# A float32 layer pair on one core: an interleaved order for the last two units' second products, and another refinement of the inverse square root

## What is computed

```python
# layer 1
approx_up = x @ up_w.T                              # 128 columns
delta = x @ gate_w.T - local_point
out = approx_up @ local_approx_output.T + sum over m = 1..6 of
      (delta**m / m! * approx_up) [m > 4: only where |delta| <= 2.5] @ fuse_weight[:, :, m-1].T
out += (silu(x @ ffn_gate_w.T) * (x @ ffn_up_w.T)) @ ffn_down_w.T      # 1248 inner columns
x = layernorm(x + out)                              # (x - mean) / sqrt(var + 1e-5)
# layer 2
inter = x @ c1_w.T @ c2_w.T                         # 1792 columns in 56 blocks of 32
idx = argmax in each block                          # one row of w1 and w2t is chosen per block
x = layernorm(x + relu(x @ w1[idx].T) @ w2t[idx])
```

## Time and profile before

| | us |
|---|---|
| median of 3 executions | 782.3 (782.02 to 784.47) |
| the profiled execution, as a whole | 782.61 |
| its span | 780.7 |
| TensorE (PE) busy | 753.7 |
| VectorE (DVE) busy | 480.8 |
| ScalarE (ACT) busy | 226.4 |
| GpSimd (POOL) busy | 159.4 |
| mean granted TensorE clock | 0.996 of full |

### The profile page before, as it was taken

One profiled execution on the slowest core, in us unless ns is written; L12 is line 12 of the kernel. 1 busy time (PEld: TensorE's weight loads), 2 busy tenths in 40 slices (PEclk: granted clock), 3 DMA queues, 4 the chain that ended last, 5 costly groups with the idle time before them and its releaser, 6 DMA issues.

```text
span 780.7 us, 12799 instructions
## 1 busy us (share of the span) xinstructions
PE 753.7 (97%) x3814; PEld 356.6 (46%) x3814; DVE 480.8 (62%) x854; ACT 226.4 (29%) x356; POOL 159.4 (20%) x132
## 2 busy tenths in 40 slices
PE   7999999999999999999999999999999999999994
PEld 2444443444444444444444444454545444444441
DVE  4888677697867777767967786445654561034105
ACT  1644456437432222222122222221222222112220
POOL 0444433111111111111111112212211221222210
PEclk9999999999999999999999999999999999999998
DMA  8446328210000000000000000000100010001001
GB/s 324 173 163 200 55 53 302 77 54 1 1 1 0 0 1 0 0 0 0 0 3 0 0 1 1 1 1 1 54 0 0 0 55 0 0 1 55 0 0 54
DMA packets 9341, 31.81 MB, mean 41 GB/s; under 512 B 992, under 2 KB 1632, under 8 KB 8416
## 3 DMA queue, kind: packets, MB, share of 16 engines
q1 hardware_dynamic: 7200, 27.22, 9.2%
q0 software_dynamic: 2112, 4.19, 3.2%
HBM read 27.22 MB, written 4.19 MB: 40 GB/s over the span
## 4 chain that ended last, share of the span: by engine, by line
PE 83%; DVE 8%; issue 3%; ACT 2%; DMA 1%; SPq 1%; DVEq 0%; ACTq 0%; POOL 0%
PE acc L366 28%; PE pa L354 19%; PE pb L354 19%; PE acc L431 9%; PE pick_b L462 1%; DMA big<-in_x_t 1%; DVE big L1229 1%; PE pick_a L452 1%; PE pick_a L414 1%; DVE big L943 1%; DVE small L1155 1%; PE pa L568 1%; ACT big L788 1%; PE pick_a L470 1%; PE pb L568 1%
## 5 line engine op out<-in xcount | busy, mean ns | idle before, releaser
L366 PE MATMUL acc<-big,work 128*128 128x512 f16 (+1 forms) x1128 | 254.6, 379 | 0.0
L853 POOL TENSOR_TENSOR work<-work 128x512 f32 (+1 forms) x96 | 115.9, 1207 | 533.1 <-ACT work L759 287.9
L354 PE MATMUL pa<-xs,big 128*128 128x512 f16 (+1 forms) x816 | 187.3, 379 | 5.1 <-issue 3.1
L354 PE MATMUL pb<-xs,big 128*128 128x512 f16 (+1 forms) x816 | 187.2, 379 | 2.2 <-DVE work L1138 2.1
L366 PEld LDWEIGHTS acc<-big,work 128*128 (+1 forms) x1128 | 108.6, 98 | 123.4 <-issue 0.3
L354 PEld LDWEIGHTS pa<-xs,big 128*128 128x128 f16 (+1 forms) x816 | 78.7, 98 | 99.8 <-issue 7.9
L354 PEld LDWEIGHTS pb<-xs,big 128*128 128x128 f16 (+1 forms) x816 | 78.8, 98 | 92.9 <-issue 4.1
L1328 DVE TENSOR_TENSOR big<-rev,winner 128x1024 bf16<-128x1024 f16 x28 | 34.1, 1219 | 76.6 <-PE pb L568 76.6
L431 PE MATMUL acc<-big 128*128 128x512 f16 x336 | 73.7, 379 | 0.6 <-POOL big L860 0.6
L826 ACT ACTIVATE work<-pa 128x512 f32<-128x512 f32 x28 | 16.7, 597 | 180.1 <-PE pa L568 180.1
L759 ACT ACTIVATE work<-work 128x512 f32 (+1 forms) x40 | 25.2, 630 | 114.7 <-DVE work L1138 114.7
(11 more groups left out here) (136 smaller groups left out, 613.8 us busy)
## 6 DMA issues: line engine op xcount, KB each, us to landing
big<-in_w_all SPq DMA_DIRECT2D x2, 3840.0 KB, 16.8
big<-in_x_t SPq DMA_DIRECT2D x16, 256.0 KB, 4.0
rows<-in_x POOLq DMA_DIRECT2D x4, 1024.0 KB, 9.4
big<-in_w_all SPq DMA_DIRECT2D x2, 1536.0 KB, 9.9
out<-rows SPq DMA_DIRECT2D x3, 1024.0 KB, 4.4
big<-in_w_all SPq DMA_DIRECT2D x1, 2048.0 KB, 16.6
big<-in_w_all SPq DMA_DIRECT2D x2, 1024.0 KB, 5.8
big<-in_fuse_t SPq DMA_DIRECT2D x2, 768.0 KB, 7.5
```

The lines of the kernel that those rows point to most:

```text
L354: mm = nc.tensor.matmul(dst[:, :], weights(wp)(kc * P, P), x_part16(g, xp, kc), start=(kc == 0 and wp == xp), stop=(stop and kc == KC - 1 ...
L366: mm = nc.tensor.matmul(acc[t][:, :], act_part(pair, j, ap, t * P, P), weights(wp)(0, H), start=(first and ap == wp), stop=(last and ap == 1))
L853: nc.gpsimd.tensor_tensor(act_part(pair, j, 1), act32[j], act_part(pair, j, 0), ALU.subtract).then_inc(act_lo, 1)
```

## The change

Two edits. On TensorE the second products of the last two units (5 and 6 of group 3) are no longer issued as 24 chunk by chunk, and then 24 tile by tile. Unit 6 leaves the loop: its first products and masks are written out behind it (`unit2(3, U2 - 1, ..., "none")`), and then eight pieces of 6 matmuls follow, each one tile of one unit, in the order (5, 0), (5, 1), (5, 2), (6, 0), (6, 1), (5, 3), (6, 2), (6, 3). The last of each tile signals as before. PE waits for the parts of each chunk ahead of the first piece of its unit.

On VectorE the two bit steps are kept. The three Newton steps (9 instructions) become one third-order step of 4 instructions, whose result is left unscaled, and one Newton step of 3, whose constants (`CUBE`) take in the scale: 7 instead of 9, in all eight normalisations.

```diff
--- before.py
+++ after.py
@@ -587,7 +587,8 @@
                         if j == 0:
                             after_third()
                     return
-                second2(g, u, kind, after_third)
+                if kind != "none":
+                    second2(g, u, kind, after_third)
 
             pe.wait_ge(w2_lo, 2 * C2 + 4)
             pe.wait_ge(silu_ready, N1)
@@ -630,19 +631,27 @@
                         unit2(g + 1, 0, s(tile, 3), none, none, "last")
             for g in (2, 3):
                 unit2(g, 1, none, none, none, "first")
-                with pe.Fori(2, U2) as u:
+                with pe.Fori(2, U2 if g == 2 else U2 - 1) as u:
                     unit2(g, u, none, none, none, "middle")
                 if g == 2:
                     unit2(3, 0, none, none, none, "last")
 
-            before = GROUPS * U2 - 1
-            pe.wait_ge(act_lo, N1 + before * 2 + 2)
-            for t in range(TPG):
+            def second_tile(unit, t, done=False):
+
                 for j in range(2):
+                    if t == 0:
+                        pe.wait_ge(act_lo, N1 + unit * 2 + j + 1)
                     for ap, wp in ((0, 0), (0, 1), (1, 0)):
-                        mm = nc.tensor.matmul(acc[t][:, :], act_part(before + GROUPS * U1, j, ap, t * P, P),
-                                              w2_part(C2 - 2 + j, 1, wp)(0, H), start=False, stop=(j == 1 and ap == 1))
-                mm.then_inc(sparse_ready, 1)
+                        mm = nc.tensor.matmul(acc[t][:, :], act_part(unit + GROUPS * U1, j, ap, t * P, P),
+                                              w2_part((unit % U2) * 2 + j, 1, wp)(0, H), start=False,
+                                              stop=(done and j == 1 and ap == 1))
+                if done:
+                    mm.then_inc(sparse_ready, 1)
+
+            LAST_UNIT = GROUPS * U2 - 1
+            unit2(3, U2 - 1, none, none, none, "none")
+            for unit, t in ((1, 0), (1, 1), (1, 2), (0, 0), (0, 1), (1, 3), (0, 2), (0, 3)):
+                second_tile(LAST_UNIT - unit, t, unit == 0)
 
 
         @block.scalar
@@ -1170,19 +1179,30 @@
                 settle()
                 step(v.tensor_scalar(y_.bitcast(I32), ya_.bitcast(I32), -1.0, float(0x5F3759DF), ALU.mult, ALU.add))
                 settle()
-                for _ in range(NEWTON):
-                    step(v.scalar_tensor_tensor(out=ya_, in0=y_, scalar=-0.5, in1=y_, op0=ALU.mult, op1=ALU.mult))
+                def size(factor):
+
+                    step(v.scalar_tensor_tensor(out=ya_, in0=y_, scalar=factor, in1=y_, op0=ALU.mult, op1=ALU.mult))
                     settle()
                     step(v.tensor_tensor(ya_, ya_, ve_, ALU.mult))
                     settle()
-                    step(v.scalar_tensor_tensor(out=y_, in0=ya_, scalar=1.5, in1=y_, op0=ALU.add, op1=ALU.mult))
+
+                def refine(term):
+
+                    step(v.scalar_tensor_tensor(out=y_, in0=ya_, scalar=term, in1=y_, op0=ALU.add, op1=ALU.mult))
                     settle()
+
+                size(1.0)
+                step(v.scalar_tensor_tensor(out=ya_, in0=ya_, scalar=-10.0 / 3.0, in1=ya_, op0=ALU.add, op1=ALU.mult))
+                settle()
+                refine(5.0)
+                size(-0.5 * CUBE ** 3)
+                refine(1.5 * CUBE)
                 for t in tiles:
                     v.tensor_scalar(row(g, t), row(g, t), mv[:, t, 0:1], y[:, t:t + 1],
                                     ALU.subtract, ALU.mult).then_inc(signal, 1)
 
-            NEWTON = 3
-            NORM_STEPS = 2 * TPG + 3 + 3 * NEWTON
+            CUBE = 3.0 / 8.0
+            NORM_STEPS = 2 * TPG + 3 + 7
 
             def x1_low(tile):
                 dve.wait_ge(x1_hi, tile + 1)
```

## The result

| | median, us | executions | profiled execution's span |
|---|---|---|---|
| before | 782.56 (781.66 to 784.85) | 18 | 780.7 |
| changed | 780.64 (779.76 to 781.90) | 18 | 778.9 |

The ratio is 0.9973, with a 95% interval of 0.9966 to 0.9979: about 2.1 us less (1.6 to 2.7), and the forecast was 2.24. Of the executions of the kernel before beside which e5 to e8 ran, one took 1342.86 us at a mean granted clock of 0.558; it is left out of their ratios.

The account below looks back on a forecast made before the run. TensorE was taken to bound most of the run, VectorE its tail; 1.04 us (tile order) plus three times 0.40 (refinement) makes 2.24, from 782.3 to 780.06 us, range 779.2 to 781.8.

Parts of the forecast that it names:

- The order: Tail of the last group: interleaved second products let VectorE take tile 3 at 770.32 instead of 771.36, 1.04 us gained.
- the lag of 0.20: Tail: VectorE started tile 0 0.20 us after its 30th matmul; the same lag was assumed for the new order.
- The cover of GpSimd's wait: Before piece (6,0) at 763.13: GpSimd's low part for chunk 1 is done at 762.05, leaving 1.1 us of cover.
- The refinement: Two fewer small instructions give 0.40 us each at the end, in group 1 and at the start of phase 2.
- only the tail counts: Rival, chance 0.14: in the two places in the middle another release ends last, so 1.44 us gained, 780.9 us.
- The instruction held while GpSimd subtracts: Group 1: a small instruction lasting 1.02 us would be the ninth of ten and held the same, so 0.40 stays.
- More comes back: Rival, chance 0.15: the loop's dropped round gives 0.62 us, or group 1's held instruction escapes, 0.86 at most; 779.4 or 779.2.
- "Nothing" for the other five normalisations: The other five normalisations lie beside a TensorE that doesn't wait, so shortening them gains nothing.
- The written-out unit at nothing: Group 3's loop: writing out one round keeps the same 32 first products and masks in order, costed at nothing.
- The chances: Whole run: faster beyond the border 0.40, within 0.3% 0.55, slower 0.05.
- the border of 0.3%: Whole run: about 0.3%, here 2.35 us, is what a measurement of this kernel can tell from no change.

Follow-up runs that it names:

- e5: The changed kernel with the seven instructions refining the inverse square root left out (3 small instructions instead of 10): 778.27 us, ratio 0.9940 to the kernel before.
- e8: The changed kernel with each tile's two pieces together, (5,0), (6,0), (5,1), (6,1) and so on: 780.89 us, ratio 0.9974 to the kernel before.
- e1: The kernel before with the interleaved order alone, keeping its three Newton steps: 781.94 us, ratio 0.9987.
- e2: The kernel before with the shorter refinement alone, in the order of before: 781.62 us, ratio 0.9982.
- e4: The changed kernel's order with six Newton steps, 21 small instructions instead of the 12 before, in each of eight normalisations: 794.35 us, ratio 1.0152 to the kernel before.
- e3: The kernel before with only the last unit written out behind the loop, product order and refinement as before: 783.03 us, ratio 1.0002.

## Why the prediction was right

- **The order, 1.04 us:** 1.01 (e1). The working was by two rates, 0.216 us a matmul and 1.81 us a tile, and the lag of 0.20; the third take, which waits for TensorE, fell on its hundredth. The 0.03 is VectorE's: behind a wait its tile takes 1.84 us instead of 1.81 (769.97 - 768.13).
- **The cover of GpSimd's wait, 1.1 us:** there was no gap (the tail's row of 48). The prediction had the cover too small, though. It put the wait for both parts ahead of piece (6,0), but the kernel waits for chunk 1 only ahead of that chunk's matmuls, the 22nd of the 48. By the 0.216 us a matmul that is at 763.40, and GpSimd is done at 760.52 + 1.16 = 761.68: 1.7 us of cover. e8 shows what happens without it: all the lateness goes to TensorE, 0.9 us, and 0.38 of it to the last take.
- **The refinement, three times 0.40:** 0.39 at the end and 0.40 and 0.39 in the middle (e2, and the changed kernel). e5 shows that the two waits give until they are used up, e4 that they take all that is added. The rival "only the tail counts" fell with e2 and e4.
- **The instruction held while GpSimd subtracts:** it stayed the ninth and left the gain as it was. *More comes back* fell.
- **"Nothing" for the other five normalisations:** right for fewer instructions. It holds in one direction only: e4 found 1.6 and 1.5 us of waits in groups 2 and 3, where the row before had stood 0 to 0.03 us off a wait.
- **The written-out unit at nothing:** e3, 1.0002. The Trainium skill (page "Runtime: NRT & Kernel Launch", section "Instruction fetch mechanics") states that a taken branch outside the fetched window stalls, and that this is one reason why kernels prefer unrolling. e3 neither bears this out nor speaks against it: this loop had no gap to give back, and no run shows whether its branch leaves that window.
- **The chances:** the ratio 0.9973 lies just within the border of 0.3%, as was the forecast (0.29% less); its interval reaches across it, so no side of that border is shown.
- **The time itself:** 780.06 was forecast and 780.64 measured. About 0.26 of this comes from the start of the sum, the median of before: 782.3 from three executions, 782.56 from eighteen. The rest lies within the interval.

On the small instructions the Trainium skill (page "VectorE: DVE Perf Modes", section "Rules for kernel authors") advises to minimise the count of chained instructions rather than their semaphores. On the count the runs agree: with 3, 10, 12 and 21 of them in the last normalisation, each with its wait, one costs 0.20 us, on 4 elements a partition. No run took a wait away.

## What to carry to other kernels

When the last engine in line works tile by tile, the work ahead of it should complete tiles at its rate, early for the first and just in time for the rest: take both rates from the tail's rows, write down when each tile is complete and when it can be taken, and place every piece by that. A cut in a chain of small dependent instructions pays once at every place where a busy engine waits behind that chain, up to the wait that is there, and nowhere else; the list of waits gives both the places and the caps. Before lengthening such a chain, look for places that stand just off a wait.

## What the runs showed of the hardware that was not expected

- The part of the run up to the first feed-forward product varied from 113.3 (e5) to 115.8 us (e8) between profiled executions with the same instructions there, while the distances behind it that an edit doesn't touch repeated to 0.1 us. The spans differ by as much as this study's effects.
- In the profile of e8 the granted TensorE clock was 0.55 from 16 to 18 us and 0.60 from 18 to 20, so for most of that time at the lower of its two levels (1.2 instead of 2.4 GHz); in the other nine profiles it was 1.00 there. TensorE had stood still for 2.22 us for a transfer just before, but in e1 for 3.0 without a fall. From the start of the eight matmuls at 16.30 to the row behind them it is 5.16 us instead of the 3.97 in the kernel before, which is 1.2 of the 1.6 us that e8 is late at its first feed-forward product. What lowered the clock no run shows.

```profile
16.30 5.33 PE L414 MATMUL pick_a<-big 128*128 128x512 f32 x8 [2.22 <-DMA big<-in_x_t]
```

- The scatter of whole executions goes with the mean granted clock. Of the 42 executions of the kernel before that the ratios of e1 to e8 use, the twelve of 784.12 us or more have 0.993, the other thirty 0.994 to 0.996.
- The idle time in the brackets of a TensorE row is 0.16 or 0.17 us short of what the wait costs, by e5, where 0.84 and 0.43 were worth 1.01 and 0.59.
- In e4, a wait of 0.2 us cost TensorE another 0.30 us after it, twice, both times in the first round of the short loops of groups 2 and 3, with the next products right behind the mask. Being in a hardware loop is not enough for it: the waits ahead of the mask at 477.90 in the changed kernel (0.43 us) and at 565.94 in e4 (0.80) lie in the loop over groups 0 and 1, and the transposes behind them followed after 0.23 us, without such a gap. What the engine does in that time the trace doesn't tell.
- A small VectorE instruction that starts while GpSimd's 128 x 512 subtraction runs lasts until that is over: 1.02 us instead of 0.16 in group 1. The changed kernel's trace has this at four normalisations, where the small instruction starts 0.09 to 0.25 us after the subtraction: it lasts 1.02, 1.01, 1.08 and 0.93 us, and ends 0.01 to 0.03 us after it each time. Without a small one there, the hold of about 0.84 us fell on the scalings (e5). That GpSimd is the cause is read from this coincidence of the ends; no run took GpSimd's work away.
